# Selective-scan strand of a four-layer kernel: decay into PSUM, products on GpSimd, halved scans, new banks and orders

## The chip, the cores and the metric

One Trainium2 chip, one core. The metric is the device time of one execution in microseconds, median of the runs shown. TensorE is PE in the rows, VectorE DVE, ScalarE ACT, GpSimd POOL, and SP issues the DMAs. All arithmetic is in float32, except the rows that add a bias in a product (bfloat16 parts).

## The reference, cut to what matters

Four layers in a row over x of 32 batches x 256 steps x 256 channels. L0 and L3 are linear attention with FiLM, L1 is softmax attention with 16 heads of 16, and L2 has two selective scans, the second over reversed time:

```python
delta = softplus(einsum(dlt, Wdt) + bdt)              # batch, 256 steps, 512 channels
dA  = exp(delta[..., None] * A)                       # ... x 16 states
dBu = delta[..., None] * Bm[:, :, None, :] * u[..., None]
def step(h, xs):                                      # one step of time
    h = dA_t * h + dBu_t
    y = einsum('ben,bn->be', h, C_t)
...
out = einsum((y1 + y2) * silu(mx), Wf) + bf + skip
return x + gate * out
```

A, dBu and y are what the change touches: 2 scans x 512 channels x 16 states x 256 steps per batch, 32 batches.

## The kernel before, in words

A setup part turns the weights once (until about 150 us). Then one block runs 32 batches as four strands, each a generator per engine whose `yield` ends a step:

- **A** (L0, then L1; `pe_linear`, `pe_softmax` and their like on each engine) is one serial chain per batch. L1 makes scores of two heads at a time ("s0" to "s7", L368), VectorE takes their maxima (L425), then the scores come again transposed ("st0" to "st7", L389), ScalarE takes exponentials (L466) and TensorE multiplies with v (L398). A has PSUM banks 0 to 2 and one buffer A_x.
- **C** (first half of L2; `c_pe`, `c_dve`, `c_act`, `c_pool`): norms, projections, softplus; L559 finishes delta, L658 makes delta * u. It stores delta and delta * u in DRAM (dd) and B and C rows (bc). Banks 3 and 4.
- **S** (the scans; `s_*`). The loads of `load_slot` bring dd back, each channel on four partitions. A batch has 32 units u = (channel block c of 4, direction s of 2, q of 4); a unit is 128 partitions (32 channels x 4 states) by 4 lines of 256 steps. Per unit: ScalarE writes the decay exp(delta * A) to the buffer S_dA, 255 of 256 elements per line so that a zero stays where a line starts (four instructions, L682); VectorE writes the product B * (delta * u) to PSUM banks 6 and 7 (L702) and scans all 1024 elements in one instruction to the buffer X (L710); GpSimd multiplies X by C in place (L730), once VectorE is past the B product of the next unit; TensorE sums over states into bank 5 (L751). After 8 units VectorE gates the sum (L719). X has four places.
- **T** (end of L2, then L3; `t_*`): the product with wf, L786 and L790 on VectorE, then L3 as L0. It uses buffers of C (dd, xh, tmp) and so waits in `last_c` for C of two batches later. Banks 3 and 4, shared with C.

Each engine has one written list of letters, ORDER (L906), which is one turn: `program` (L915) takes one step of the strand that each letter names. In a turn A works on batch b + 2, C on b + 1, S on b and T on b - 1. Engines execute their lists in order, and semaphores hold them together. All DMAs are issued by SP in a list of its own.

L275 is the last write of a layer: A_x<-ps,A_ring ends L0, A_x<-ps,A_x ends L1, xs<-ps,xs ends L3.

## Time and profile before

| | |
|---|---|
| three runs | 5470.70, 5474.84, 5478.48 us (median 5474.84) |
| span of the profiled execution | 5460.8 us |
| what lies around the span, against the median | 14 us |
| busy: PE, PEld, DVE | 4205.5, 2715.4, 4723.7 us |
| busy: ACT, POOL | 3712.5, 3038.3 us |
| mean granted TensorE clock | 0.814 |

The profiled execution's own time is given as its span, from the first to the last instruction. Busy shares count instructions that run; matmuls are pipelined, so a busy PE is not PE at its peak. A float32 matmul has two records. An idle time in a row is charged to the instruction that ended the wait.

### The profile page before, as it was taken

How to read it: one execution, taken by the hardware profiler on the slowest of the kernel's cores; microseconds unless marked ns; L12 is line 12 of the kernel's file. 1: busy time of each engine (PE TensorE's matmuls, PEld its weight loads, DVE VectorE, ACT ScalarE, POOL GpSimd, SP SyncE). 2: the span in 40 equal slices, each digit the busy share in tenths (PEclk: the TensorE clock that was granted, in tenths of full speed). 3: DMA queues.
4: the chain of work that ended last, by engine and by line, in shares of the span. 5: the costliest groups of instructions: out<-in, count | busy, mean ns of one | idle time of the engine just before them, and what ended most of it. 6: DMA issues, size and time to landing. Idle time of an engine off the chain costs nothing.

```text
span 5460.8 us, 71238 instructions
## 1 busy us (share of the span) xinstructions
PE 4205.5 (77%) x25876; PEld 2715.4 (50%) x25876; DVE 4723.7 (87%) x4533; ACT 3712.5 (68%) x8614; POOL 3038.3 (56%) x1388
## 2 busy tenths in 40 slices
PE   5677787788878877888787778878877888788655
PEld 4444455555545555555455555555555555455423
DVE  4217999999999999999999999999999999999986
...
DMA packets 321199, 462.13 MB, mean 85 GB/s; under 512 B 55457, under 2 KB 148777, under 8 KB 320845
## 3 DMA queue, kind: packets, MB, share of 16 engines
...
q14 instruction: 150, 1.23, 0.1%
...
## 4 chain that ended last, share of the span: by engine, by line
PE 42%; DVE 40%; issue 6%; ACT 6%; POOL 3%; DVEq 0%; DMA 0%; SPq 0%; POOLq 0%; ACTq 0%
PE ps L164 21%; DVE S_X L710 20%; DVE ps L702 10%; PE ps L751 5%; PE ps L389 4%; PE ps L368 4%; DVE A_sm L425 3%; PE ps L524 3%; POOL S_X L730 3%; PE ps L154 2%; ACT S_dA L682 2%; DVE A_raw L129 1%; PE ps L398 1%; DVE T_raw L129 1%; ACT A_ring L147 1%
## 5 line engine op out<-in xcount | busy, mean ns | idle before, releaser
L730 POOL TENSOR_TENSOR S_X<-S_X,S_bc 128x1024 f32<-128x1024 f32 x1024 | 2442.5, 2386 | 1738.5 <-DVE ps L702 1738.3
L710 DVE TENSOR_TENSOR_SCAN S_X<-S_dA,ps 128x1024 f32<-128x1024 f32 x1024 | 2337.8, 2283 | 73.1 <-PE ps L751 1.0
L682 ACT ACTIVATE S_dA<-S_slot,acol 128x255 f32<-128x255 f32 x4096 | 1706.9, 495 | 275.8 <-DVE S_X L710 275.8
L702 DVE TENSOR_TENSOR ps<-S_slot,S_bc 128x1024 f32<-128x1024 f32 x1024 | 1337.3, 1306 | 27.6
L751 PE MATMUL ps<-S_X,sum 128*32 128x256 f32 x8192 | 732.9, 463 | 76.6 <-POOL S_X L730 73.7
L154 PE MATMUL ps<-ident,A_ring 128*128 128x128 f32 x768 | 189.7, 405 | 486.6 <-ACT A_ring L147 375.3
L751 PEld LDWEIGHTS ps<-S_X,sum 128*32 128x32 f32 x8192 | 218.2, 123 | 427.1 <-issue 253.3
L368 PE MATMUL ps<-A_kP,A_qP 32*128 32x256 f32 x2048 | 338.1, 453 | 119.1 <-DVE A_sm L425 119.1
L154 PEld LDWEIGHTS ps<-ident,A_ring 128*128 128x128 f32 x768 | 131.1, 205 | 566.0 <-ACT A_ring L147 426.5
L466 ACT ACTIVATE A_ring<-ps 128x1024 f32<-128x1024 f32 x256 | 261.5, 1021 | 188.5 <-PE ps L389 188.5
L425 DVE TENSOR_REDUCE A_sm<-ps 128x4 f32<-128x1024 f32 x256 | 311.8, 1218 | 48.6 <-PE ps L368 36.2
L389 PE MATMUL ps<-A_qP,A_kP 32*128 32x256 f32 x2048 | 335.8, 451 | 20.7 <-ACT A_ring L466 12.3
L368 PEld LDWEIGHTS ps<-A_kP,A_qP 32*128 32x128 f32 x2048 | 196.6, 207 | 251.2 <-DVE A_sm L425 192.9
L164 PE MATMUL ps<-C_xT,wcz 128*128 128x256 f32 x1024 | 296.3, 441 | 1.8 <-ACT C_dd L600 1.8
L658 POOL TENSOR_TENSOR C_dd<-C_dd 128x1024 f32<-128x1024 f32 x64 | 179.2, 2801 | 190.0 <-DVE C_dd L559 190.0
L389 PEld LDWEIGHTS ps<-A_qP,A_kP 32*128 32x128 f32 x2048 | 199.0, 209 | 144.6 <-issue 100.4
L164 PEld LDWEIGHTS ps<-C_xT,wcz 128*128 128x128 f32 x1024 | 220.6, 227 | 61.5 <-issue 12.6
L746 PE MATMUL ps<-C_xT,wD 128*128 128x256 f32 x512 | 166.1, 456 | 77.3 <-DVE S_g L719 73.2
L138 ACT ACTIVATE A_nm<-A_mv 128x2 f32<-128x2 f32 x128 | 26.0, 203 | 266.3 <-DVE A_mv L132 266.3
L164 PE MATMUL ps<-wf,S_g 128*128 128x256 f32 x512 | 198.7, 570 | 4.8 <-DVE S_X L710 2.4
L398 PE MATMUL ps<-A_ring,A_vA 128*32 128x256 f32 x2048 | 162.9, 443 | 37.8 <-ACT A_ring L466 37.8
L460 ACT ACTIVATE A_ring<-ps 16x256 f32<-16x256 f32 x32 | 11.9, 372 | 253.2 <-PE ps L375 253.2
...
## 6 DMA issues: line engine op xcount, KB each, us to landing
S_slot<-scr_dd SPq DMA_DIRECT2D x1024, 256.0 KB, 4.6
...
S_bc<-scr_bc SPq DMA_DIRECT2D x256, 256.0 KB, 5.3
...
```

The source lines that it names most:

```text
L154: ins = p.transpose(bank[:, col * 256 + r * P:col * 256 + (r + 1) * P], src[:, r, col * P:(col + 1) * P], ident[:])
L164: ins = p.matmul(out, l, r, start=n == 0, stop=n == len(terms) - 1)
L368: ins = p.matmul(bank[o][:, t * 256:(t + 1) * 256], B["qP"][r, g, t * P:(t + 1) * P], B["kP"][r, g, :], start=True, stop=True, tile_positi ...
L389: ins = p.matmul(bank[o][:, t * 256:(t + 1) * 256], B["kP"][r, g, t * P:(t + 1) * P], B["qP"][r, g, :], start=True, stop=True, tile_positi ...
L398: ins = p.matmul(bank[2][PADH * i:PADH * (i + 1), g % 2 * 256:(g % 2 + 1) * 256], B["vA"][:, t, 4 * g + i, :], B["ring"][:, 4 * (g % 2) + ...
L425: v.tensor_reduce(B["sm"][:, :, 2 * n:2 * n + 2].rearrange("p t h -> p h t"), B["pair"].rearrange("p h (t m) -> p h t m", t=TT), AX, ALU.m ...
L466: a.activation(B["ring"][:, 2 * (n % 4):2 * (n % 4) + 2, :], B["pair"], ACT.Exp).then_inc(S.act.sem, 1)
L682: ins = a.activation(B["dA"][:, s, q % 2, j, lo:lo + T - 1], B["slot"][:, s, j, 0, lo:lo + T - 1], ACT.Exp, scale=K.k["acol"][:, s, 4 * c ...
L702: v.tensor_tensor(B["in"], B["slot"][:, s, :, 1, :], rep(B["bc"][:, s, q, :], 1, 4), ALU.mult).then_inc(S.dve.sem, 1)
L710: v.tensor_tensor_scan(line(X[:, u % 4]), line(B["dA"][:, s, q % 2]), line(B["in"]), 0.0, ALU.mult, ALU.add).then_inc(S.dve.sem, 1)
L730: g.tensor_tensor(B["X"][:, u % 4], B["X"][:, u % 4], rep(B["bc"][:, s, NQ + q, :], 1, 4), ALU.mult).then_inc(S.pool.sem, 1)
L751: ins = p.matmul(B["bank"][32 * j:32 * j + 32, (c % 2) * T:(c % 2 + 1) * T], K.k["sum4"][:], B["X"][:, u % 4, j, :], start=False, stop=las ...
```

## The change

- **Scan (s_act, s_dve).** ScalarE writes the decay of half a unit (two lines of 256) straight into one of three PSUM banks (5, 6, 7), used in a ring. There is no zero column kept any more: GpSimd sets the first delta of each line to 1e30 before dd is stored (event far), and A is held at or above 3e-28, so that the exponential there is 0. VectorE scans each half by itself (512 elements).
- **Products.** GpSimd makes all 32 B products into X, now a ring of 8. In odd units (ON_POOL) VectorE scans X in place and GpSimd makes the C product over 1024 elements, queued behind the B product of two units later (POOL_LAG). In even units VectorE scans in place in the PSUM bank and makes the C product itself, 512 elements at a time, into X.
- **Banks.** A has 0 and 1, C has 2, T has 3, the state sums 4, the decay ring 5 to 7. The waits that a shared bank needs move with that. In L1 the products with v are made two groups at a time, after e3 and e7. In L0 and L3 the row sums and the reciprocal of q move ahead of y.
- **T** has buffers of its own; `last_c` is gone.
- **Orders.** The strands run on over all batches (`batches`), each engine's list is a long FIRST and then a repeated TURN. A turn has 100 steps of S on VectorE, 24 of A, 11 of T and 4 of C; on GpSimd 48, 2, 1 and 8. In VectorE's FIRST the 100th step of S, the last of batch 0, stands behind 2.83 batches of A's steps, one batch of C's and none of T's; the same distances hold at the end of each S.
- S_sp and s_sp wait for GpSimd's b instead of VectorE's, and the load of bc for the last sum instead of the last C product. The number of DMAs stays.

Core of the diff:

```diff
 UNITS, SLOTS = 32, 8
+LINES, RING, SCAN_BANKS = 4, 8, 3
+ON_POOL = frozenset(range(1, UNITS, 2))
+GATE_LAG, POOL_LAG = 2, 2
+FAR = 1e30
 ACT_SET = "natural_log_exp_and_others"
-
-AHEAD = {"A": 2, "C": 1, "S": 0, "T": -1, "a": 3, "s": 1, "t": -1}
...
-BANKS = {"L0": {"xT": 0, "q": 1, "k": 2, "v": 0, "kT": 2, "qT": 1, "att": 0, "y": 2, "hT": 1, "o": 0},
-         "L1": {"hT": 2, "o": 0},
-         "L3": {"xT": 0, "q": 1, "k": 0, "v": 1, "kT": 0, "qT": 1, "att": 0, "y": 1, "hT": 0, "o": 1}}
+BANKS = {"L0": {"xT": 0, "q": 1, "k": 0, "v": 1, "kT": 0, "qT": 1, "att": 0, "y": 1, "hT": 0, "o": 1},
+         "L1": {"hT": 0, "o": 1},
+         "L3": {n: 0 for n in ("xT", "q", "k", "v", "kT", "qT", "att", "y", "hT", "o")}}
...
     yield
+    if L == "L3":
+        p.wait_ge(S.dve.sem, S.dve.at(b, "qsub"))
     for c in range(KD):
         ins = matmuls(p, bank["k"][:, c * 256:(c + 1) * 256], [(k[L + "wk"][:, i, c * P:(c + 1) * P], B["xT"][:, i, :]) for i in range(KD)]
                       + [(k["bias"][:, K.at[L + "k"]][:, c * P:(c + 1) * P], B["om" + L][:])])
     ins.then_inc(S.pe.sem, 1)
     yield
     if L == "L3":
+        p.wait_ge(S.act.sem, S.act.at(b, "kexp1"))
+    else:
         p.wait_ge(S.dve.sem, S.dve.at(b, "qsub"))
     project(p, bank["v"], B["xT"], k[L + "wv"], bias("v"), k["ones"], S.pe)
     yield
-    p.wait_ge(S.act.sem, S.act.at(b, "kn1" if L == "L0" else "kexp1"))
+    p.wait_ge(S.act.sem, S.act.at(b, "kn1" if L == "L0" else "v1"))
     turn_tiles(p, k["ident"], B["ke"], bank["kT"], S.pe)
     yield
...
-    p.wait_ge(S.act.sem, S.act.at(b, "kT"))
+    H = P // dh
+    p.wait_ge(S.act.sem, S.act.at(b, "qT"))
+    for t in range(TT):
+        for c in range(KD):
+            at = 256 + (t * KD + c) * H
+            p.matmul(bank["att"][:, at:at + H], B["xT"][:, c, t * P:(t + 1) * P], k["same%d" % dh][:, 0:P:dh], start=True, stop=True)
     lhs, rhs = (B["v"], B["kT"]) if L == "L0" else (B["kT"], B["v"])
     for c in range(KD):
         ins = matmuls(p, bank["att"][:, c * P:(c + 1) * P], [(lhs[:, t, c * P:(c + 1) * P], rhs[:, t, c * P:(c + 1) * P]) for t in range(TT)])
     ins.then_inc(S.pe.sem, 1)
     yield
-    p.wait_ge(S.dve.sem, S.dve.at(b, "bd1"))
-    p.wait_ge(S.act.sem, S.act.at(b, "qT"))
+    p.wait_ge(S.dve.sem, S.dve.at(b, "qrec"))
     for t in range(TT):
         for c in range(KD):
             ins = p.matmul(bank["y"][:, t * D + c * P:t * D + (c + 1) * P], B["xT"][:, c, t * P:(t + 1) * P], B["bd"][:, c, :], start=True, stop=True)
-
-    H = P // dh
-    for t in range(TT):
-        for c in range(KD):
-            at = 256 + (t * KD + c) * H
-            ins = p.matmul(bank["att"][:, at:at + H], B["xT"][:, c, t * P:(t + 1) * P], k["same%d" % dh][:, 0:P:dh], start=True, stop=True)
...
+            bk = bank[1 - half]
             for c in range(2):
                 f = slice((2 * half + c) * P, (2 * half + c + 1) * P)
                 last = (k["bias"][:, K.at["L1" + m]][:, f], k["ones"][:] if m == "q" else B["omL1"][:])
                 ins = matmuls(p, bk[:, c * 256:(c + 1) * 256], [(k[L + "w" + m][:, i, f], B["xT"][:, i, :]) for i in range(KD)] + [last])
             ins.then_inc(S.pe.sem, 1)
     yield
-    p.wait_ge(S.act.sem, S.act.at(b, "q1"))
-    project(p, bank[2], B["xT"], k[L + "wv"], k["bias"][:, K.at[L + "v"]], k["ones"], S.pe)
+    p.wait_ge(S.dve.sem, S.dve.at(b, "k0"))
+    project(p, bank[1], B["xT"], k[L + "wv"], k["bias"][:, K.at[L + "v"]], k["ones"], S.pe)
 
     for n in range(PAIRS):
         yield
         p.wait_ge(S.dve.sem, S.dve.at(b, "m%d" % (n - 1) if n else "k1"))
+        if n == 0:
+            p.wait_ge(S.act.sem, S.act.at(b, "v1"))
...
-    for n in range(PAIRS + 1):
-        if n < PAIRS:
+    for n in range(PAIRS):
+        yield
+        if n == 0:
+            p.wait_ge(S.act.sem, S.act.at(b, "max"))
+            p.wait_ge(K.land["max"].sem, K.land["max"].at(b))
+        else:
+            p.wait_ge(S.act.sem, S.act.at(b, "yT0" if n == 4 else "e%d" % (n - 1)))
+        for t in range(TT):
+            for g, i, o in heads(n):
+                r = slice(PADH * i, PADH * (i + 1))
+                ins = p.matmul(bank[o][:, t * 256:(t + 1) * 256], B["kP"][r, g, t * P:(t + 1) * P], B["qP"][r, g, :],
+                               start=True, stop=True, tile_position=(PADH * i, 0))
+        ins.then_inc(S.pe.sem, 1)
+        if n % 4 == 3:
             yield
-            if n == 0:
-                p.wait_ge(S.act.sem, S.act.at(b, "max"))
-                p.wait_ge(K.land["max"].sem, K.land["max"].at(b))
...
-            for t in range(TT):
-                for i in range(4):
-                    ins = p.matmul(bank[2][PADH * i:PADH * (i + 1), g % 2 * 256:(g % 2 + 1) * 256], B["vA"][:, t, 4 * g + i, :],
-                                   B["ring"][:, 4 * (g % 2) + i, t * 256:(t + 1) * 256], start=t == 0, stop=t == TT - 1,
-                                   tile_position=(0, PADH * i), skip_group_check=True)
+            p.wait_ge(S.act.sem, S.act.at(b, "e%d" % n))
+            for g in (n // 2 - 1, n // 2):
+                for t in range(TT):
+                    for i in range(4):
+                        ins = p.matmul(bank[0][PADH * i:PADH * (i + 1), g % 2 * 256:(g % 2 + 1) * 256], B["vA"][:, t, 4 * g + i, :],
+                                       B["ring"][:, 4 * (g % 2) + i, t * 256:(t + 1) * 256], start=t == 0, stop=t == TT - 1,
+                                       tile_position=(0, PADH * i), skip_group_check=True)
             ins.then_inc(S.pe.sem, 1)
...
         g.tensor_tensor(B["dd"][:, :, 1, :], B["dd"][:, :, 1, :], B["dd"][:, :, 0, :], ALU.mult).then_inc(S.pool.sem, 1)
+        g.wait_ge(S.pool.sem, S.pool.at(b, "du%d" % s))
+        g.memset(B["dd"][:, :, 0, (T - 1) * s:(T - 1) * s + 1], FAR).then_inc(S.pool.sem, 1)
...
 def s_act(a, K, b):
     S, B = K.S["S"], K.Sb
     for u in range(UNITS):
-        yield
-        m, c, s, q = u // 4, u // 8, (u // 4) % 2, u % 4
-        lo = 1 - s
-        if q == 0:
-            a.wait_ge(K.land["slot%d" % s].sem, K.land["slot%d" % s].at(b, 4 * (c + 1)))
-        if q >= 2:
-            a.wait_ge(S.dve.sem, S.dve.at(b, "scan%d" % (u - 2)))
-        elif u >= 6:
-            a.wait_ge(S.dve.sem, S.dve.at(b, "scan%d" % (u - 6)))
-        elif b:
-            a.wait_ge(S.dve.sem, S.dve.at(b - 1, "scan%d" % (u - 6 + UNITS)))
-        for j in range(4):
-            ins = a.activation(B["dA"][:, s, q % 2, j, lo:lo + T - 1], B["slot"][:, s, j, 0, lo:lo + T - 1], ACT.Exp, scale=K.k["acol"][:, s, 4 * c + j, q:q + 1])
-        ins.then_inc(S.act.sem, 1)
+        c, s, q = u // 8, (u // 4) % 2, u % 4
+        for i in range(2):
+            yield
+            if q == 0 and i == 0:
+                a.wait_ge(K.land["slot%d" % s].sem, K.land["slot%d" % s].at(b, 4 * (c + 1)))
+            before = 2 * (UNITS * b + u) + i - SCAN_BANKS
+            if before >= 0:
+                bb, ub, ib = before // (2 * UNITS), before // 2 % UNITS, before % 2
+                a.wait_ge(S.dve.sem, S.dve.at(bb, ("scan%d_%d" if ub in ON_POOL else "c%d_%d") % (ub, ib)))
+            for n in range(2):
+                j = 2 * i + n
+                ins = a.activation(B["bank"][half_at(b, u, i)][:, n * T:(n + 1) * T], B["slot"][:, s, j, 0, :], ACT.Exp,
+                                   scale=K.k["acol"][:, s, LINES * c + j, q:q + 1])
+            ins.then_inc(S.act.sem, 1)
 
 
 def s_dve(v, K, b):
     S, B = K.S["S"], K.Sb
-    X = B["X"]
-    for w in range(UNITS + 2):
+    two = lambda ap: ap.rearrange("p (j t) -> p j t", t=T)
+    for w in range(UNITS + GATE_LAG):
         if w < UNITS:
             u, c, s, q = w, w // 8, (w // 4) % 2, w % 4
-            line = lambda ap: ap.rearrange("p j t -> p (j t)")[:, ::-1] if s else ap.rearrange("p j t -> p (j t)")
+            line = lambda ap: ap[:, ::-1] if s else ap
+            for i in range(2):
+                decay, x = B["bank"][half_at(b, u, i)], B["X"][:, u % RING, 2 * i:2 * i + 2, :]
+                out = x.rearrange("p j t -> p (j t)") if u in ON_POOL else decay
+                yield
+                if i == 0:
+                    v.wait_ge(S.pool.sem, S.pool.at(b, "b%d" % u))
+                v.wait_ge(S.act.sem, S.act.at(b, "exp%d_%d" % (u, i)))
+                v.tensor_tensor_scan(line(out), line(decay), line(x.rearrange("p j t -> p (j t)")), 0.0, ALU.mult, ALU.add).then_inc(S.dve.sem, 1)
+                if u not in ON_POOL:
+                    yield
+                    if u in (0, 4):
+                        v.wait_ge(K.land["bc%d" % s].sem, K.land["bc%d" % s].at(b))
+                    v.wait_ge(S.dve.sem, S.dve.at(b, "scan%d_%d" % (u, i)))
+                    v.tensor_tensor(x, two(decay), rep(B["bc"][:, s, NQ + q, :], 1, 2), ALU.mult).then_inc(S.dve.sem, 1)
+        if w >= GATE_LAG and (w - GATE_LAG) % 8 == 7:
             yield
...
 def s_pool(g, K, b):
     S, B = K.S["S"], K.Sb
-    for u in range(UNITS):
-        yield
-        s, q = (u // 4) % 2, u % 4
-
-        g.wait_ge(S.dve.sem, S.dve.at(b, "b%d" % (u + 1) if u + 1 < UNITS else "scan%d" % u))
-        g.tensor_tensor(B["X"][:, u % 4], B["X"][:, u % 4], rep(B["bc"][:, s, NQ + q, :], 1, 4), ALU.mult).then_inc(S.pool.sem, 1)
+    for w in range(UNITS + POOL_LAG):
+        if w < UNITS:
+            u, c, s, q = w, w // 8, (w // 4) % 2, w % 4
+            yield
+            if q == 0:
+                g.wait_ge(K.land["slot%d" % s].sem, K.land["slot%d" % s].at(b, 4 * (c + 1)))
+            if u in (0, 4):
+                g.wait_ge(K.land["bc%d" % s].sem, K.land["bc%d" % s].at(b))
+            if u >= RING:
+                g.wait_ge(S.pe.sem, S.pe.at(b, "sum%d" % (u - RING)))
+            elif b:
+                g.wait_ge(S.pe.sem, S.pe.at(b - 1, "sum%d" % (u - RING + UNITS)))
+            g.tensor_tensor(B["X"][:, u % RING], B["slot"][:, s, :, 1, :], rep(B["bc"][:, s, q, :], 1, LINES), ALU.mult).then_inc(S.pool.sem, 1)
+        u = w - POOL_LAG
+        if u in ON_POOL:
+            s, q = (u // 4) % 2, u % 4
+            yield
+            g.wait_ge(S.dve.sem, S.dve.at(b, "scan%d_1" % u))
+            g.tensor_tensor(B["X"][:, u % RING], B["X"][:, u % RING], rep(B["bc"][:, s, NQ + q, :], 1, LINES), ALU.mult).then_inc(S.pool.sem, 1)
...
-        p.wait_ge(S.pool.sem, S.pool.at(b, "c%d" % u))
+        if u in ON_POOL:
+            p.wait_ge(S.pool.sem, S.pool.at(b, "c%d" % u))
+        else:
+            p.wait_ge(S.dve.sem, S.dve.at(b, "c%d_1" % u))
...
-def last_c(e, K, b):
-
-    S, c = K.S["C"], min(b + 2, NB - 1)
-    e.wait_ge(S.pool.sem, S.pool.at(c, "gate"))
-    e.wait_ge(K.land["dd_out1"].sem, K.land["dd_out1"].at(c))
-
-
```

BANKS of L0, `dve_softmax` and `act_softmax` follow the banks above. C waits for the copy out of its one bank ahead of each product; the first product of T waits for the end of the T before. The strings of FIRST and TURN are left out.

## Rows read from the trace of the kernel before

**Rows 1.** The page, busy time, share of the span and instructions of each engine.

```profile
PE 4205.5 (77%) x25876; PEld 2715.4 (50%) x25876; DVE 4723.7 (87%) x4533; ACT 3712.5 (68%) x8614; POOL 3038.3 (56%) x1388
```

**Rows 2.** Busy us (instructions) of PE, PEld, DVE, ACT, POOL by stretch; clock, DMA, GB/s.

```profile
620.00:2190.00 1570.00, 1261.31 (x7940) 816.15 (x7940) 1444.83 (x1351) 1156.73 (x2691) 949.34 (x431) 0.84 0.38 89
2190.00:3760.00 1570.00, 1259.21 (x7941) 816.09 (x7941) 1445.76 (x1351) 1157.13 (x2690) 949.71 (x431) 0.84 0.38 89
```

**Rows 3.** Line L275 between 2300 and 2800 us: ns min/median/max, first and last start.

```profile
L275 DVE TENSOR_TENSOR A_x<-ps,A_x x4: 691/692/692, 2309.3 to 2780.3; 128x512 f32<-128x512 f32 x4
```

**Rows 4.** Line L275 over the whole span.

```profile
L275 DVE TENSOR_TENSOR A_x<-ps,A_x x32: 690/692/693, 300.3 to 5135.5; 128x512 f32<-128x512 f32 x32
L275 DVE TENSOR_TENSOR xs<-ps,xs x32: 691/691/693, 736.5 to 5457.6; 128x512 f32<-128x512 f32 x32
```

**Rows 5.** Timeline of VectorE (start us, us, engine, line): three single writes.

```profile
434.72 0.69 DVE L275 TENSOR_TENSOR A_x<-ps,A_x 128x512 f32<-128x512 f32 x1 [12.08 <-PE ps L164]
...
5282.21 0.69 DVE L275 TENSOR_TENSOR xs<-ps,xs 128x512 f32<-128x512 f32 x1 [0.17 <-PE ps L164]
...
5411.49 0.69 DVE L275 TENSOR_TENSOR xs<-ps,xs 128x512 f32<-128x512 f32 x1 [0.59 <-PE ps L164]
```

**Rows 6.** The page, chain of work that ended last, by engine and by line.

```profile
PE 42%; DVE 40%; issue 6%; ACT 6%; POOL 3%; DVEq 0%; DMA 0%; SPq 0%; POOLq 0%; ACTq 0%
PE ps L164 21%; DVE S_X L710 20%; DVE ps L702 10%; PE ps L751 5%; PE ps L389 4%; PE ps L368 4%; DVE A_sm L425 3%; PE ps L524 3%; POOL S_X L730 3%; PE ps L154 2%; ACT S_dA L682 2%; DVE A_raw L129 1%; PE ps L398 1%; DVE T_raw L129 1%; ACT A_r
```

**Rows 7.** The page, costliest groups: count, busy us, mean ns, idle before and releaser.

```profile
L730 POOL TENSOR_TENSOR S_X<-S_X,S_bc 128x1024 f32<-128x1024 f32 x1024 | 2442.5, 2386 | 1738.5 <-DVE ps L702 1738.3
L710 DVE TENSOR_TENSOR_SCAN S_X<-S_dA,ps 128x1024 f32<-128x1024 f32 x1024 | 2337.8, 2283 | 73.1 <-PE ps L751 1.0
L702 DVE TENSOR_TENSOR ps<-S_slot,S_bc 128x1024 f32<-128x1024 f32 x1024 | 1337.3, 1306 | 27.6
L466 ACT ACTIVATE A_ring<-ps 128x1024 f32<-128x1024 f32 x256 | 261.5, 1021 | 188.5 <-PE ps L389 188.5
```

**Rows 8.** Who waited for whom, VectorE: us in total, times, longest.

```profile
DVE A_x L275 <- PE ps L164: 158.2, 64, 12.1
DVE C_xh L786 <- PE ps L164: 93.0, 31, 8.1
```

**Rows 9.** Single lines of VectorE over the span: ns min/median/max.

```profile
L702 DVE TENSOR_TENSOR ps<-S_slot,S_bc x1024: 1204/1232/3183, 435.3 to 5406.2; 128x1024 f32<-128x1024 f32 x171
...
L710 DVE TENSOR_TENSOR_SCAN S_X<-S_dA,ps x1024: 2266/2286/2290, 437.3 to 5408.6; 128x1024 f32<-128x1024 f32 x171
...
L790 DVE TENSOR_TENSOR xs<-xs,C_xh x32: 691/692/693, 682.5 to 5423.4; 128x512 f32<-128x512 f32 x32
```

**Rows 10.** Single lines of GpSimd, and its groups by form.

```profile
L730 POOL TENSOR_TENSOR S_X<-S_X,S_bc x1024: 2336/2357/3352, 441.0 to 5411.0; 128x1024 f32<-128x1024 f32 x171
...
L658 POOL TENSOR_TENSOR C_dd<-C_dd x64: 2343/2368/3281, 346.3 to 5215.5; 128x1024 f32<-128x1024 f32 x64
...
L1469 POOL MEMSET const-float32-1.0<- 128x1 f32 x1 | 0.1, 99 | 0.0
```

**Rows 11.** Timeline: four exponentials of ScalarE.

```profile
2509.71 1.70 ACT L682 ACTIVATE S_dA<-S_slot,acol 128x255 f32<-128x255 f32 x4 [0.45 <-DVE S_X L710]
```

**Rows 12.** Strand A undisturbed: stretches of L1 and L0, and its timeline.

```profile
207.00:300.00 93.00, 58.54 (x270) 34.66 (x270) 14.45 (x21) 19.62 (x35) 1.26 (x1) 0.59 0.01 3
300.00:336.00 36.00, 24.95 (x105) 18.83 (x104) 8.13 (x25) 19.56 (x53) 6.82 (x6) 0.74 0.05 16
...
224.27 0.84 ACT L456 ACTIVATE A_vA<-ps,A_pc 128x256 f32<-128x256 f32 x2 [5.25 <-PE ps L164]
260.19 2.07 PE L389 MATMUL ps<-A_qP,A_kP 32*128 32x256 f32 x8 [1.12 <-ACT A_ring L466]
262.19 1.93 PE L398 MATMUL ps<-A_ring,A_vA 128*32 128x256 f32 x16
264.06 2.08 PE L389 MATMUL ps<-A_qP,A_kP 32*128 32x256 f32 x8
```

More of the change, by code:

```diff
@@ L1 @@
 from contextlib import ExitStack
+from itertools import chain, cycle
 import concourse.bass as bass
@@ L347, in pe_softmax @@
     turn_tiles(p, k["ident"], B["xh"], bank[0], S.pe)
-    for m, bb in (("q", (1, 2)), ("k", (0, 1))):
+    for m in "qk":
         for half in range(2):
             yield
-            p.wait_ge(S.act.sem, S.act.at(b, "q0" if m == "k" and half else "xT"))
-            bk = bank[bb[half]]
+            p.wait_ge(S.act.sem, S.act.at(b, "q%d" % half if m == "k" else "xT"))
+            bk = bank[1 - half]
             for c in range(2):
@@ L417, in dve_softmax @@
     norm_stats(v, lambda t: x[:, t, :], B["st"], S.dve, b, [("", 0), ("", 1)])
-    for half, bk in ((0, bank[0]), (1, bank[1])):
+    for half, bk in ((0, bank[1]), (1, bank[0])):
         yield
@@ L932, in products_of_setup, with batches @@
+def batches(e, K, make):
+    for b in range(NB):
+        yield from make(e, K, b)
+def program(e, K, engine):
+    work = {letter: batches(e, K, make) for letter, make in WORK[engine].items()}
+    for strand in work.values():
+        next(strand)
+    running, order = set(work), chain(FIRST[engine], cycle(TURN[engine]))
+    while running:
+        letter = next(order)
+        if letter in running and next(work[letter], "over") == "over":
+            running.remove(letter)
 def products_of_setup():
@@ L1393, in buffers @@
     A["omL0"], A["omL1"] = sb("omL0", [P, T], BF16), sb("omL1", [P, T], BF16)
[L1394 removed]
+    A["bank"] = [ps[:, b, :] for b in (0, 1)]
     A["pair"] = ps[:, 0:2, :]
@@ L1432, in _ @@
             def _(v):
-                for q in range(2):
-                    v.memset(K.Sb["dA"][:, 0, q, :, 0:1], 0.0).then_inc(K.ready, 1)
-                    v.memset(K.Sb["dA"][:, 1, q, :, T - 1:T], 0.0).then_inc(K.ready, 1)
                 v.memset(K.A["vA"][:], 0.0).then_inc(K.ready, 1)
```

413 lines of the change are left out of this document (294 added, 119 removed).

## The prediction

> **What bounds the kernel now.** I read five views, in this order. First the busy shares [rows 1]: VectorE 87%, TensorE 77%, ScalarE 68%, GpSimd 56%. Then the busy time by stretch [rows 2]: from 620 us on, two stretches of ten turns have the same VectorE time to a microsecond, 1444.8 and 1445.8 of 1570, so a turn (one batch in each of the four strands) has one fixed length, with VectorE busy 144.5 us of it. Its length stands in the writes of x [rows 3]: four from 2309.3 to 2780.3 us, 157.0 apart. The first final output is at 736.5, the last at 5457.6 [rows 4, 5]; between them lie 28 turns of 157 (4396), then 149, 129 and 46 us, where strands have run out.
>
> The chain of waits [rows 6] says what makes a turn 157 long: 42% TensorE and 40% VectorE, of that 20% the scan L710 and 10% the product L702. This is strand A (L0 and L1 of one batch, a serial chain), standing behind scans. Last the costs by line [rows 7]: a turn has 32 scans of 2.283 and 32 B products of 1.306, 73.1 + 41.8 = 114.9 us; VectorE's other work is 144.5 - 114.9 = 29.7. The short idle times ahead of L710 and L702 are (73.1 + 27.6)/32 = 3.1. So 157 = 144.5 + 3.1 + 9.4; the 9.4 is mostly VectorE standing in its fixed order before a product of TensorE that has not come: two of its lines, L275 and L786, waited 158.2 + 93.0 us in the span for TensorE, 8 per turn [rows 8].
>
> **The change, part by part.**
>
> *VectorE.* It loses the 32 B products. It makes 64 half scans and 32 half C products (16 even units). No row has a scan of 512. A product takes 1.232 for 1024 elements and 0.692 for 512 [rows 4, 9], so 0.15 fixed and 1.05 ns per element; the same fixed part on a scan gives (2.283 + 0.15)/2 = 1.217. Ends: 1.142 (nothing fixed) and 1.30 (twice as much fixed), which is -5 and +5 us per turn. I take 1.217, since every VectorE group of two sizes has that fixed part. Sum: 64 x 1.217 + 32 x 0.692 + 29.7 = 77.9 + 22.1 + 29.7 = 129.7, where 144.5 was. Hand-overs: 96 operations instead of 64, of which 32 wait for the scan just before them; at 71 ns for one ahead of a dependent L710 that is 3.1 to 7, and I take 4.
>
> Operands in PSUM: the scan's decay now comes from PSUM and its other input from SBUF, before the other way round. A product with one input in PSUM (L275) and one with both in SBUF (L790) both take 0.692 [rows 4, 9], so I put nothing on it. The Trainium skill, "VectorE: DVE Perf Modes", section on the TRN2 errata, gives 58 cycles of fixed cost to an SBUF source and 120 to a PSUM source. By that rule the 32 C products, which read PSUM where the B products did not, would cost 65 ns more each (an estimate from the page, 2.1 us per turn, some 60 us in all); the two rows disagree with it.
>
> *VectorE against GpSimd.* B product L702 has median 1.232, mean 1.306 and a worst case of 3.183 [rows 7, 9]; L658 on GpSimd goes from 2.343 to 3.281 [rows 10]. L710, with one SBUF input, has 2.266 to 2.290 throughout [rows 9], and the C products of GpSimd that start beside one have a median of 2.357. So a VectorE instruction with two SBUF inputs and a GpSimd instruction hold each other up, one with a single SBUF input does not. The change takes the 32 two-input products away, and halves and C products have one SBUF input each. What stays is three per turn (L559 twice, L790), and GpSimd will almost always be busy then: up to one GpSimd operation (2.36) each, 0 to 7 us per turn, half of it 3.5. The Trainium skill, "SBUF — State Buffer", section "Who interferes with whom", has the same rule, as an exclusive lock on the shared port pair for the whole instruction; by it alone the price would be that of the whole lock, up to 7.
>
> *GpSimd.* 32 B products and 16 C products of 2.357 (median of L730 [rows 10]) are 113.1. Its other work is 95.0 - 32 x 2.386 = 18.6 now [rows 2, 7], where 95.0 is 949.7/10, less 1 that L658 gets back with the collisions, 17.6. The two new memsets are 0.1 each, by a small memset row [rows 10]; the other end is half a product, 1.2. Together 130.9, where 95 was. It becomes as full as VectorE.
>
> *ScalarE.* 128 exponentials of 256 instead of 255 elements; four take 1.70 now, 0.425 each [rows 11], and 1024 elements out of PSUM take 1.02 [rows 7], so between 0.26 and 0.43 at the new place. I keep 0.425 and 115.7 per turn [rows 2]; less would change nothing, since ScalarE has 30 us to spare. New is the cover: dA gave ScalarE two units or more, over 7 us; the ring of three halves lets it be at most two halves ahead, 2.4 to 3.8 us. L466 stood 188.5/32 = 5.9 us per turn behind TensorE [rows 7]; an exponential queued behind it now can be late. Bounds 0 to 5.9; I take it inside the remainder below.
>
> *TensorE and banks.* Same products, 126 us of records per turn [rows 2]. Strand A goes from three banks to two. In the undisturbed L1 of batch 0 (93 us, granted clock 0.59) [rows 12]: s0 now also waits for the v copy, +1.0. A step of st and e takes 2.08 + 1.02 + 0.1 = 3.2; with a group of y between (260.19 to 264.06) it takes 3.87, so a group cost 0.67 three times and its whole 1.93 at the end, 3.9. Now two groups come together after e3 and again after e7, 3.8 each, and yT0 (half of 1024 elements, 0.6) stands before st4: 8.2 - 3.9 = +4.3. A is 5 us longer. In L0 q's reciprocal and the row sums move ahead of y, out of the way (1 us less), and v and att wait longer for their bank (about as much): nothing. C on one bank adds eight alternations of about 1 us, T (L3) about 6 us. The last T, alone, takes 46 us [rows 4, 5], and C of batch 0 fits between 300 and 435 us beside an A; both have a whole turn, so nothing. T no longer shares C's buffers and no longer waits for C of two batches later; that can give back some of L786's 93/32 = 2.9 us per turn (0 to 2.9, I take 0). *SP queue:* same DMAs. The slot loads now wait for GpSimd's b instead of VectorE's and are wanted about four units (16 us) later. Nothing.
>
> *The sum for a turn:* VectorE 129.7 + hand-overs 4 + collisions 3.5 = 137.2, plus the remainder of 9.4 as it is = 146.6, less 0.6 for scans half as long in front of A: **146 us**. Start: A of batches 0 and 1 ends at 434.7 [rows 5], plus 10 for two longer As. The new VectorE list puts 83% of A's third batch ahead of the end of the first S, as the old one put all of it: 0.83 turn. Then one turn to the first output, 28 more, and the last three. S of batch 30 without A is bound by GpSimd (131 less A's two products) at 130, S of batch 31 (113 and T's product) at 118; the last T is 47. For turn length t: 434.7 + 10 + 29.83 t + 130 + 118 + 47 + 3 (output) + 14 = 757 + 29.83 t. The 14 is what lies around the span: 5474.8 is the median, the profiled span 5460.8. With t = 157 and no other gain this gives 5440 for 5475, because the last three stretches are shorter. With t = 146: **5112 us**, 6.6% less.
>
> **The rivals.**
> (a) *Well packed.* The remainder vanishes since scans are half as long and T is free of C: t = 138, 4874 us. For it: strand A alone takes 93 + 36 = 129 [rows 12] at a low clock, less at 0.84. Against it: VectorE 137, GpSimd 131 and A 134 would all have to fit in 138.
> (b) *Strand A is the bound.* A needs 129 + 5 by itself and waited 28 in a turn; with GpSimd's queue full and ScalarE's cover thin, only 10 of the 28 go: t = 152, 5291 us. For it: 42% of the chain on TensorE, which the change does not touch.
> (c) *GpSimd and VectorE in lockstep: slower.* GpSimd's C product waits for a scan and stands in its queue ahead of the next B, which VectorE needs; the lag is two units, 7 us. If none of GpSimd's other work (17.6) is hidden by that lag, all of it becomes idle VectorE: t = 146 + 17.6 = 163.6, 5637 us. It turns slower than now from 12.5 of the 17.6 on (t = 158.5). For it: GpSimd is at 131 of 146 and can't catch up. Against: A's reductions slow VectorE, not GpSimd, and the new lists interleave C singly.
> (d) *It brings nothing:* ring or slots starve the scan so that t stays at 157 to 158. By the shorter end alone that is 5440 to 5470 us, 0.6% faster to the same.
>
> **How the numbers follow.** Forecast 0.58 (own range t = 142 to 150: 4993 to 5232), (a) 0.15, (b) 0.18, (c) 0.06, (d) 0.03. The ends of the unknown costs (half scan -5 to +5, hand-overs -1 to +3, collisions -3.5 to +3.5, cover 0 to +5.9, T -2.9) make 138.5 to 153 if not all fall on one side: 4885 to 5325. Runs spread by 0.14%, so 0.2% is what can be told from no change. Faster 0.92 (all but (c) and a part of (d)), same 0.02, slower 0.06.
>
> **What would show it.** Half scans of 1.22 and half C products of 0.69, both steady beside GpSimd; 2.36 for B; writes of x 146 apart; VectorE at 89 to 91% and GpSimd at 88 to 90% of a turn. (a) would show as x 138 apart; (b) as VectorE idle before A's steps behind TensorE and ScalarE; (c) as VectorE idle before scans with GpSimd as the releaser; (d) with ScalarE. I would be wrong by the largest amount if GpSimd's idle time before C products and VectorE's before scans both pass 10 us per turn, or if the half scan costs over 1.3.

## The result, and the profile after

Median 5265.3 us (5261.9 to 5271.6) against 5472.8 (5463.1 to 5478.5): a ratio of 0.962, 95% interval 0.961 to 0.964. The change brings 207 us where 363 were forecast; the time lies in the stated range (4885 to 5325), outside the forecast's own range (4993 to 5232), and near rival (b)'s 5291. Below, a "turn" is the mean distance of the writes of x by strand A, from the 6th to the 32nd, in the profiled execution. Times are medians of four runs, and a_alone has a single one. One run of pe_off_chain, 9632 us at a granted clock of 0.634 where the other three have 0.815 to 0.819, is left out.

The page of the kernel after answers [rows 1, 6 and 7]: busy time by engine, the chain that ended last, and the costly groups. L711 is the scan (once for even, once for odd units), L717 VectorE's C product, L744 B and L750 C on GpSimd, L692 the exponentials, L774 the sums.

```profile
PE 4086.9 (78%) x25876; PEld 2626.4 (50%) x25876; DVE 4162.8 (79%) x5553; ACT 3681.6 (70%) x8614; POOL 4130.8 (79%) x1964
...
PE 46%; ACT 21%; DVE 13%; POOL 7%; issue 7%; DMA 2%; SPq 1%; DVEq 0%; POOLq 0%; ACTq 0%
```

```profile
L744 POOL TENSOR_TENSOR S_X<-S_slot,S_bc 128x1024 f32<-128x1024 f32 x1024 | 2396.2, 2361 | 70.7 <-DMA S_bc<-scr_bc 27.6 <-DMA S_slot<-scr_dd 25.1 <-issue 17.6
L692 ACT ACTIVATE ps<-S_slot,acol 128x256 f32<-128x256 f32 x4096 | 1731.5, 466 | 223.6 <-DVE S_X L717 183.0 <-DVE S_X L711 27.4 <-DMA S_slot<-scr_dd 9.2
L711 DVE TENSOR_TENSOR_SCAN ps<-ps,S_X 128x512 f32<-128x512 f32 x1024 | 1249.4, 1220 | 170.2 <-ACT ps L692 121.9 <-POOL S_X L744 47.6
L750 POOL TENSOR_TENSOR S_X<-S_X,S_bc 128x1024 f32<-128x1024 f32 x512 | 1218.4, 2380 | 370.3 <-DVE S_X L711 308.9 <-DMA S_bc<-scr_bc 60.2
L711 DVE TENSOR_TENSOR_SCAN S_X<-ps,S_X 128x512 f32<-128x512 f32 x1024 | 1206.6, 1206 | 53.0 <-ACT ps L692 49.4 <-POOL S_X L744 2.3 <-POOL S_X L750 0.4
L717 DVE TENSOR_TENSOR S_X<-ps,S_bc 128x512 f32<-128x512 f32 x1024 | 703.1, 687 | 34.3 <-issue 0.2
```

The busy time of two stretches of some ten turns each (as [rows 2]), and the writes of x (as [rows 4]):

```profile
1062.00:2586.00 1524.00, 1229.89 (x7948) 790.01 (x7946) 1272.75 (x1670) 1146.17 (x2688) 1289.99 (x611) 0.85 0.40 92
2586.00:4087.00 1501.00, 1215.31 (x7952) 778.87 (x7952) 1272.67 (x1674) 1147.10 (x2697) 1293.22 (x612) 0.86 0.40 93
```
```profile
L282 DVE TENSOR_TENSOR A_x<-ps,A_x x32: 666/691/693, 318.9 to 4983.9; 128x512 f32<-128x512 f32 x32
```

The two stretches are 1524 and 1501 us long: the turn now varies (146 to 161), where it was 157.0 each time [rows 3]; its mean is 150.8. That makes 20.06 turns of the 3025 us, each with VectorE busy 126.9 us, GpSimd 128.8, TensorE 121.9 and ScalarE 114.3. VectorE works 17.6 us less per turn than before and the turn is only 6.2 shorter: its idle time grew from 12.5 to 23.9. The chain has only 13% of VectorE (40% before [rows 6]), 7% of GpSimd, and 46% of TensorE.

Where VectorE's new idle time stands (waited for, us in total between 1062 and 4984 us, which is 26 turns, times, longest):

```profile
DVE S_g L726 <- PE ps L774: 140.5, 40, 8.3
DVE ps L711 <- ACT ps L692: 108.4, 84, 3.6
DVE A_sm L432 <- PE ps L377: 87.4, 113, 3.3
DVE S_X L711 <- ACT ps L692: 35.0, 36, 4.3
```

Of some 23.6 us per turn, 13.1 lie ahead of strand S's own steps (3.1 before): 5.5 are scans that wait for exponentials and 5.4 the gate L726 that waits for TensorE's sums. 8.3 lie ahead of A's steps (4.2 before).

The written orders differ too. The kernel before repeats one list each turn. The kernel after runs all 32 batches on TensorE and VectorE out of FIRST, and cut after each last step of S there, no two neighbouring turns are alike. The change thus also put irregular orders in place of a regular one; new_order below bears on that.

### The profile page after: what moved, and what is told of

The parts are those of the page before. It is cut to its first block, busy times and chain, and to the rows that moved or that the text cites. A ratio compares the mean times of both kernels' runs of the same rounds, so it can differ in the third digit from the quotient of the medians.

```text
span 5260.2 us, 72771 instructions
## 1 busy us (share of the span) xinstructions
PE 4086.9 (78%) x25876; PEld 2626.4 (50%) x25876; DVE 4162.8 (79%) x5553; ACT 3681.6 (70%) x8614; POOL 4130.8 (79%) x1964
## 4 chain that ended last, share of the span: by engine, by line
PE 46%; ACT 21%; DVE 13%; POOL 7%; issue 7%; DMA 2%; SPq 1%; DVEq 0%; POOLq 0%; ACTq 0%
PE ps L170 23%; ACT ps L692 6%; PE ps L774 5%; PE ps L396 5%; PE ps L377 4%; DVE ps L711 4%; POOL S_X L744 3%; DVE S_X L711 3%; POOL S_X L750 3%; ACT A_ring L471 2%; PE ps L405 2%; PE ps L529 2%; ACT A_ring L153 2%; PE ps L766 1%; DVE S_X L717 1%
## 5 line engine op out<-in xcount | busy, mean ns | idle before, releaser
L744 POOL TENSOR_TENSOR S_X<-S_slot,S_bc 128x1024 f32<-128x1024 f32 x1024 | 2396.2, 2361 | 70.7 <-DMA S_bc<-scr_bc 27.6
L692 ACT ACTIVATE ps<-S_slot,acol 128x256 f32<-128x256 f32 x4096 | 1731.5, 466 | 223.6 <-DVE S_X L717 183.0
L750 POOL TENSOR_TENSOR S_X<-S_X,S_bc 128x1024 f32<-128x1024 f32 x512 | 1218.4, 2380 | 370.3 <-DVE S_X L711 308.9
L711 DVE TENSOR_TENSOR_SCAN ps<-ps,S_X 128x512 f32<-128x512 f32 x1024 | 1249.4, 1220 | 170.2 <-ACT ps L692 121.9
L711 DVE TENSOR_TENSOR_SCAN S_X<-ps,S_X 128x512 f32<-128x512 f32 x1024 | 1206.6, 1206 | 53.0 <-ACT ps L692 49.4
L774 PE MATMUL ps<-S_X,sum 128*32 128x256 f32 x8192 | 704.6, 453 | 125.3 <-POOL S_X L750 118.2
L717 DVE TENSOR_TENSOR S_X<-ps,S_bc 128x512 f32<-128x512 f32 x1024 | 703.1, 687 | 34.3 <-issue 0.2
L396 PE MATMUL ps<-A_qP,A_kP 32*128 32x256 f32 x2048 | 391.4, 513 | 197.7 <-ACT A_ring L471 97.8
L774 PEld LDWEIGHTS ps<-S_X,sum 128*32 128x32 f32 x8192 | 218.2, 121 | 464.9 <-issue 215.3
L396 PEld LDWEIGHTS ps<-A_qP,A_kP 32*128 32x128 f32 x2048 | 231.2, 241 | 365.1 <-ACT A_ring L471 170.0
L160 PE MATMUL ps<-ident,A_ring 128*128 128x128 f32 x768 | 141.2, 319 | 326.1 <-ACT A_ring L153 320.0
L377 PE MATMUL ps<-A_kP,A_qP 32*128 32x256 f32 x2048 | 302.7, 414 | 55.7 <-DVE A_sm L432 50.3
L662 POOL TENSOR_TENSOR C_dd<-C_dd 128x1024 f32<-128x1024 f32 x64 | 150.8, 2357 | 191.3 <-DVE C_dd L563 191.3
L377 PEld LDWEIGHTS ps<-A_kP,A_qP 32*128 32x128 f32 x2048 | 182.2, 191 | 161.4 <-DVE A_sm L432 84.7
L726 DVE SCALAR_TENSOR_TENSOR S_g<-ps,bD,wa 128x256 f32<-128x256 f32 x128 | 60.1, 469 | 174.5 <-PE ps L774 174.3
L170 PE MATMUL ps<-A_ring,L1wq 128*128 128x256 f32 x512 | 180.9, 493 | 13.5 <-ACT A_ring L455 13.2
## 6 DMA issues: line engine op xcount, KB each, us to landing
T_gate<-scr_mod SPq DMA_DIRECT2D x32, 128.0 KB
```

The costliest lines, as they stand in the source:

```text
L160: ins = p.transpose(bank[:, col * 256 + r * P:col * 256 + (r + 1) * P], src[:, r, col * P:(col + 1) * P], ident[:])
L170: ins = p.matmul(out, l, r, start=n == 0, stop=n == len(terms) - 1)
L377: ins = p.matmul(bank[o][:, t * 256:(t + 1) * 256], B["qP"][r, g, t * P:(t + 1) * P], B["kP"][r, g, :], start=True, stop=True, tile_positi ...
L396: ins = p.matmul(bank[o][:, t * 256:(t + 1) * 256], B["kP"][r, g, t * P:(t + 1) * P], B["qP"][r, g, :], start=True, stop=True, tile_positi ...
L692: ins = a.activation(B["bank"][half_at(b, u, i)][:, n * T:(n + 1) * T], B["slot"][:, s, j, 0, :], ACT.Exp, scale=K.k["acol"][:, s, LINES * ...
L711: v.tensor_tensor_scan(line(out), line(decay), line(x.rearrange("p j t -> p (j t)")), 0.0, ALU.mult, ALU.add).then_inc(S.dve.sem, 1)
```

## Where a turn goes, counted along strand A

For this one view I took all records of TensorE, ScalarE, VectorE and GpSimd that touch A's tiles and laid them end to end: the time in which some engine works on A, and between two such times the gap ahead of A's next instruction. In a gap its engine is either busy for another strand (A stands behind it) or idle. Over some 24 to 26 turns of each trace, per turn:

```
                     before   after   new_order (below)
turn                  157.0   151.1   146.8
A worked on           106.9   111.6   114.1
A behind TensorE       24.2    21.0    18.4
A behind VectorE       12.2     4.7     5.7
A behind ScalarE        4.8     6.8     3.4
A behind GpSimd         1.5     0.5     0.2
gaps, engine idle       7.4     6.6     5.0
```

In both kernels A is always at work or next in a queue whose engine is busy, but for 7 us. By itself this does not show that A is the bound, since the parts add up to the turn for any strand. The same count along strand S, from the same records of the kernel after, gives 141.1 worked on, 8.3 behind others and 1.5 idle. What the count gives is prices, which the experiments can test. The change took 7.5 us of standing behind VectorE's scans and B products, 3.2 behind TensorE and 1.0 behind GpSimd, put 2.0 on behind ScalarE, and A's own work grew by 4.7; idle gaps lost 0.8. That is -5.8, the whole of the gain. Of the 4.7, 1.7 is TensorE's own time on A (57.5 to 59.2) and 3.0 is overlap between engines that is gone. One place from TensorE's and ScalarE's timelines of the kernel after (start, length):

```profile
3012.88 1.60 PE L396 MATMUL ps<-A_qP,A_kP 32*128 32x256 f32 x8
3014.41 3.72 PE L170 MATMUL ps<-wf,S_g 128*128 128x256 f32 x16
3017.97 1.03 PE L766 MATMUL ps<-C_xT,wD 128*128 128x256 f32 x4
3018.93 1.93 PE L405 MATMUL ps<-A_ring,A_vA 128*32 128x256 f32 x32
```
```profile
3014.53 1.03 ACT L471 ACTIVATE A_ring<-ps 128x1024 f32<-128x1024 f32 x1 [2.46 <-PE ps L396]
```

A's exponentials are ready at 3015.56; the product y (L405) starts at 3018.93, since strand T's first product and strand S's L766 stand ahead of it. No "wait" shows this: TensorE is busy all the time.

## The experiments

Theories: (1) A's chain with its queueing sets the turn; (2) GpSimd and VectorE in lockstep; (3) TensorE's total work; (4) the ring of three halves. All kernels start from the kernel after. The first five leave work out, in turn on A, on VectorE, on GpSimd, on ScalarE, and on the last three together. Turns come from one profiled execution, times from the median, and the two can differ: over 29.83 turns, 1 us per turn is 30 us.

**a_half.** `B["pair"]...[:, :, :, 0:128]` in the maxima, `ring[..., 0:256] <- pair[..., 0:256]` in the exponentials, and both halves of y read `ring[..., 0:256]`.

> The kernel after, with strand A's eight maxima (L1) over 512 instead of 1024 elements and its eight exponentials over 512 instead of 1024, so half of the keys are left out; TensorE's products, all orders and all other strands are as they are. This takes 8 x 0.61 + 8 x 0.45 = 8.5 us per turn out of A's serial chain, 4.9 of it from VectorE's work and 3.6 from ScalarE's. Theory 1 (A's chain sets the turn): the turn falls from 150.8 by 6 to 9 us, time 4997 to 5086 us. Theory 2 (GpSimd and VectorE in lockstep through scans and B products): GpSimd's 130 us are not touched, VectorE's only by 4.9, so 0 to 4.9 us per turn, 5119 to 5265 us. Theory 3 (TensorE's own work and queue): 0, 5250 to 5270 us.

Measured 5176.9 us (0.947 of before, 0.945 to 0.949), turn 148.3: 2.5 of the 8.5 us come off. Theory 3 falls (the turn moves with TensorE's work unchanged). The size misses theory 1 and lies in theory 2's range, so this run alone does not decide between them; the next two do. That A gives less than its own saving is seen along A: standing behind TensorE rose from 21.0 to 25.3.

**dve_light and pool_light.**

```
-  v.tensor_tensor_scan(line(out), line(decay), line(x), 0.0, ...)
+  v.tensor_tensor_scan(line(out[:, 0:T]), line(decay[:, 0:T]), line(x[:, 0:T]), 0.0, ...)
```
```
-  g.tensor_tensor(X[:, u % RING], X[:, u % RING], rep(bc, 1, LINES), ALU.mult)
+  g.tensor_tensor(X[:, u % RING, 0:2], X[:, u % RING, 0:2], rep(bc, 1, 2), ALU.mult)
```

> The kernel after, with each half scan over one of its two lines (256 elements instead of 512), the other line left unscanned; nothing else is changed. VectorE's work falls by 64 x 0.54 = 34 us per turn, from 127 to 93; A's chain has no scan in it, only stands behind some. Theory 1 (A's chain): the turn falls only by what A's VectorE steps waited for the scan ahead of them, 0 to 5 us, 5116 to 5265 us. Theory 2 (lockstep): GpSimd's C products wait 309 us in the span for scans, 10 per turn, and the turn can come down to GpSimd's 131 plus a few: 134 to 142 us, 4760 to 5000 us. Theory 3 (TensorE): 5200 to 5265.

> The kernel after, with the C products of GpSimd over two of their four lines (512 elements instead of 1024), the other two left out. GpSimd's work falls by 16 x 1.1 = 18 us per turn, from 130 to 112. Theory 1 (A's chain): 0 to 3 us per turn, 5175 to 5265 us. Theory 2 (lockstep): most of GpSimd's 18 us come off the turn, 10 to 18, 4730 to 4970 us. Theory 3 (TensorE): 5200 to 5265.

Measured 5200.1 us, turn 149.4: VectorE's busy time fell by 32 us per turn, worth 1.4 (2.2 by the medians); and 5234.3 us, turn 149.8: GpSimd's fell by 17, worth 1.0. Nearly half of the scans' work gone and 99% of the turn left: neither engine alone is the bound. Both times also lie in theory 3's range, so they say nothing against TensorE.

**act_light.** One exponential for both lines: `a.activation(bank as (2, 256), slot[:, s, j:j + 2, 0, :], Exp, scale=acol of line j)`.

> The kernel after, with one exponential of 512 elements for each half (the second line takes the first one's factor) instead of two of 256: ScalarE's 64 x 2 x 0.466 become 64 x about 0.72, 13 us per turn less of 115, and each half is ready 0.2 us sooner. Theory 1 (A's chain, with ScalarE's A steps standing behind exponentials): 1 to 4 us per turn, 5146 to 5235 us. Theory 4 (the ring of three halves: scans that wait for exponentials, 171 us in the span, set the turn): 4 to 6 us per turn, 5086 to 5146 us. Theories 2 and 3: 5235 to 5265.

Measured 5187.3 us, turn 148.5: 2.3 us per turn, theory 1's range; theory 4 asked for 4 to 6. Along A, standing behind ScalarE fell from 6.8 to 4.4, which is all of it. ScalarE's busy time fell by 11 us. This is the thin cover that the prediction put at nothing.

**three_light.** The three together.

> The kernel after, with dve_light, pool_light and act_light together: VectorE 93, GpSimd 112, ScalarE 102 us per turn, TensorE and strand A as they are. Theory 1 (A's chain with TensorE's queue): three engines freed by 13 to 34 us each give no more than what A stood behind them; alone two of them gave 2.2 and 1.0 us per turn, together 4 to 9: 4997 to 5146 us. Theory 2 (lockstep of any two or three of VectorE, GpSimd and ScalarE, which no single one of them frees): 15 us per turn or more, under 4820 us.

Measured 5066.0 us, turn 146.2: 4.6 us per turn, the sum of the three alone (1.4 + 1.0 + 2.3 = 4.7). The profiled execution is the slowest of the four here (5086); by the medians it is 6.7, against 5.8 for the sum. Either way no pair of them holds the turn jointly: 62 us of the three engines' busy time are gone, and the 15 us or more that theory 2 asked for do not come. Theory 2 falls.

**pe_on_chain, pe_off_chain.** Less TensorE work, once inside A (one of two terms in A's `project` and q, k products, `for t in range(1)` in y), once outside (`if j % 2: continue` in the sums, one of two terms in wcz and wx).

> The kernel after, with less TensorE work on strand A's chain: its projections q, k, v and o (L0 and L1) over one of two halves of the contraction, the products y of L1 over one of two halves of the keys. By the groups of the profile after this takes 466/32 = 14.6 us per turn of TensorE out, all of it in A. Theory 1 (A's chain): the turn falls by a third of that or more, as when A's maxima and exponentials were halved (8.5 us out of A gave 3.0 per turn), 5 to 12 us: 4907 to 5116 us. Theory 2 (VectorE and GpSimd in lockstep): 0 to 1, 5235 to 5265. Theory 3 (TensorE's work in all, wherever it is): as much as pe_off_chain by the microsecond.

> The kernel after, with less TensorE work outside strand A: two of the four sums of each unit left out (strand S), the products with wcz and wx over one of two halves of the contraction (strand C). By the groups of the profile after this takes 552/32 = 17.3 us per turn of TensorE out, none of it in A. Theory 1 (A's chain): only what A's products stood behind others in TensorE's order, 0 to 4 us per turn, 5146 to 5265 us. Theory 3 (TensorE's work in all): 17.3/14.6 of what pe_on_chain gains. Theory 2 (lockstep): 0 to 1, 5235 to 5265.

Measured 5144.2 us, turn 147.5 (3.3 for 14.6 us) and 5192.2 us, turn 148.3 (2.5 for 17.3 us). By the work left out, a microsecond is worth 0.23 on the chain and 0.14 off it (0.28 and 0.14 by the medians). The first is outside theory 1's range; part of the reason is that the granted clock fell with the work, from 0.835 to 0.802 over the span (0.818 in pe_off_chain). TensorE's busy time on the two pages is 3866.2 and 3969.7 us for 4086.9: only 221 of 466 us and 117 of 552 really went. By that measure a microsecond of TensorE is worth no more on the chain (0.48) than off it (0.68), and in both places more than one of any other engine. Theory 3 as it stands is out by a_half, but that TensorE's queue as a whole, and not A's part of it, weighs most is not excluded.

**a_light.** a_half and pe_on_chain together.

> The kernel after, with a_half and pe_on_chain together: 8.5 + 14.6 = 23.1 us per turn out of strand A's chain (half of the elements of its maxima and exponentials, half of the contraction of its projections and y products); the other strands as they are. Theory 1 (A's chain sets the turn, other engines only where A stands behind them): the two gains add, 3.0 + 4.1 = 7.1 us per turn or more: 4980 to 5080 us. Rival (below about 146 the turn is held by VectorE with GpSimd, as the forecast had it): the second gain is mostly lost, 3.5 to 5 us in all, 5115 to 5160 us.

Measured 5047.2 us, turn 144.6: 6.2 us per turn, where the two alone gave 2.5 + 3.3. They add up, and by the medians too (7.3 against 3.0 + 4.1); 23 us taken out of A move the turn more than 62 us taken out of the three others, 218 us of time against 199. But they are 23 us by count: the time in which A is worked on fell by 17.4, to 94.1, and its standing behind other strands rose by 11. The rival (VectorE with GpSimd holds at 146) falls.

**a_alone.** Only strand A in the table of strands, x written out from A.

> Strand A alone (L0 and L1 of all 32 batches, written out as they are): strands C, S and T are left out, so nothing stands in any queue ahead of A. It shows how long one A takes when undisturbed. Setup ends near 170 us. Theory 1 (A is the bound): 125 to 140 us per batch, so 32 of them take 4180 to 4660 us in all; the 151 of the kernel after would hold only 11 to 26 us of waiting for other strands. Theory 2 (lockstep of the others) or 3 (TensorE's total): A alone takes under 115 us, under 3850 us in all, and has over 35 us of slack in a turn. The granted clock can be lower than beside the other strands; what this costs is to be read from TensorE's rows.

Measured 4553.8 us. Line L282 and a stretch of it (busy by engine, granted clock):

```profile
L282 DVE TENSOR_TENSOR A_x<-ps,A_x x32: 690/692/692, 310.3 to 4548.8; 128x512 f32<-128x512 f32 x32
```
```profile
1000.00:4000.00 3000.00, 1759.52 (x7693) 1116.56 (x7692) 464.25 (x831) 697.57 (x1445) 55.49 (x44) 0.60 0.02 4
```

(4548.8 - 310.3)/31 = 136.7 us for one A at a granted clock of 0.60; the prediction had 129 + 5, at 0.59 in L1 and 0.74 in L0. TensorE's part of it is 79.5 us here and 59.2 beside the other strands at 0.86, so an undisturbed A at that clock would take about 116 (an estimate from the two traces). A waits some 35 us per turn, not 17. The time is in theory 1's range, but read at that clock the run does not decide: 116 and 35 of slack are about what theories 2 and 3 asked for.

**pool_lag3.** `GATE_LAG, POOL_LAG = 2, 3`.

> The kernel after, whole computation, with GpSimd's C product of a unit put three units behind its B product instead of two, in the same places of the order. Theory 2 (lockstep: GpSimd stands 309 us in the span before C products for scans): this wait goes, 2 to 8 us per turn, 5030 to 5205 us. Theory 1 (A's chain): the wait moves elsewhere on GpSimd or becomes idle time, and sums on TensorE come 3.6 us later: 5235 to 5300 us.

Measured 5426.9 us (0.993 of before), turn 156.6: 5.7 us longer, almost the whole gain lost, and more than any theory gave. Who waits for GpSimd's C product, in the kernel after and here (us, times, longest):

```profile
PE ps L774 <- POOL S_X L750: 118.2, 57, 8.1
```
```profile
PE ps L774 <- POOL S_X L750: 319.1, 136, 9.6
```

The 200 us more are 6.3 per turn of TensorE standing at a sum, in order. Along A, idle gaps grew by 2.6 per turn, nearly all of them on TensorE, standing behind TensorE by 1.7 and A's own work by 1.5. GpSimd's own wait for scans did go, as theory 2 said (309 to 128 us), and it was worth nothing.

**a_split.** Whole computation; each step of A's L1 becomes two of one bank, so that TensorE writes bank 1 while VectorE or ScalarE reads bank 0.

```
-  for t in range(TT):
-      for g, i, o in heads(n): matmul(bank[o][...t...])
-  ins.then_inc(S.pe.sem, 1)
+  for g, i, o in heads(n):
+      wait m(n - 1, o)
+      for t in range(TT): matmul(bank[o][...t...])
+      ins.then_inc(S.pe.sem, 1)
```

> The kernel after, whole computation, with each step of A's L1 (scores of two heads in two banks, one maximum or exponential over both) made as two steps of one bank each, in the same place of every order: TensorE fills bank 1 while VectorE or ScalarE reads bank 0. VectorE's work grows by 8 x 0.15 = 1.2 us per turn, ScalarE's by 8 x 0.2 = 1.6, TensorE's is the same or a little more. Theory 1 (A's chain): a step alone falls from about 3.2 us to 2.3 or so, 16 steps; with other strands' instructions queued between, a part of these 14 us: 4 to 11 us per turn, 4937 to 5146 us. Theory 2 (lockstep of GpSimd and VectorE): VectorE is 1.2 us fuller, 5265 to 5300. Theory 3 (TensorE's work): 5265 to 5290.

Measured 5252.9 us (0.960, 0.959 to 0.962), turn 151.1: 12 us faster in all, none of it in the turn, and in no theory's range. The scores of A's L1 in the kernel after and here:

```profile
L396 PE MATMUL ps<-A_qP,A_kP 32*128 32x256 f32 x2048 | 391.4, 513 | 197.7 <-ACT A_ring L471 97.8 <-DMA A_qP<-A_ring 79.0 <-ACT A_kP L476 18.8
```
```profile
L396 PE MATMUL ps<-A_qP,A_kP 32*128 32x256 f32 x2048 | 440.7, 510 | 144.8 <-DMA A_qP<-A_ring 78.0 <-ACT A_ring L473 47.8 <-ACT A_kP L478 17.3
```

One record takes as long as before and the group takes 49 us more (L377 29 more): two heads' products that alternated between banks ran partly at once, and in this order they do so less. Along A, the overlap between engines grew by some 3 us per turn and the engines' work on A by as much (2.3 of it TensorE's), so that its length stayed (111.5 and 111.9).

**new_order.** Whole computation, no instruction changed; only the written orders.

```
-  FIRST = {"PE": "...ASATCATSCSSSASCCASCASASAASAASCASTCACSACS...", ...}
+  FIRST = {"PE": "...AACSACATCSSTACSCACSSTSASAAAAACSACSACSSACS...", ...}
```

> The kernel after, whole computation, not an instruction changed, added or removed: only the five written orders in which the strands' steps are issued are new. They are made by giving each engine, whenever it is free, the step that could start first by the durations of the profile after, with 0.26 us of preference for strand A on VectorE, 0.46 on ScalarE and 1.4 on GpSimd, and 0.2 against strand T on VectorE. Theory 1 (a turn is A's own 111.6 us and what A stands behind other strands' steps, 39.6 in the kernel after, which is a matter of the orders): the standing falls by 8 to 16 us per turn, until GpSimd's 130 and VectorE's 127 busy us leave little room: turn 135 to 143, time 4790 to 5030 us. Rival (the busy engines' shared load makes A stand behind others however it is ordered): the turn stays at 148 to 154, 5180 to 5360 us. If orders made from mean durations do not survive the spread of the real ones, it is slower than the kernel after.

Measured 5139.3 us (0.940, 0.938 to 0.942): 2.4% faster than the kernel after, the fastest here. Its chain and a stretch of ten turns:

```profile
PE 29%; POOL 22%; DVE 16%; ACT 14%; issue 8%; DMA 6%; SPq 2%; POOLq 0%; ACTq 0%; DVEq 0%
```
```profile
1041.00:2509.00 1468.00, 1269.89 (x7942) 799.85 (x7941) 1276.75 (x1672) 1151.76 (x2691) 1299.22 (x611) 0.84 0.41 95
```

All turns are within 0.5 us of 146.8, and standing and idle gaps along A fell from 39.6 to 32.6, so how long A stands depends on the orders. Time and turn lie between the ranges of theory 1 (135 to 143) and the rival (148 to 154), and neither is borne out: the standing fell by 7, where 8 to 16 were expected. These orders repeat one turn, where those of the kernel after differ from turn to turn; whether the repetition or the new places gave the 2.4% was not separated. TensorE's busy time rose from 121.9 to 127.0 per turn at a clock of 0.84, and what else keeps the turn at 146.8 was not separated either.

## Why the prediction was right, and where it was short

The time lies in the stated range, and largely by luck. The range reached 5325 because unit costs might all come out high. None of VectorE's and GpSimd's did. What came was more idle time on VectorE, which the sum held constant.

- *VectorE 129.7 + 3.5 for collisions:* 126.9 measured. The half scan took 1.22 and 1.21 (1.217 forecast), the half C product 0.687 (0.692). *Hand-overs 4:* the idle time ahead of scans and C products that no other engine ended is 1.1 per turn. With it VectorE comes to 128.0, where the sum had 137.2.
- *Operands in PSUM, nothing:* right for the forecast's purpose. The 65 ns that follow for a PSUM source from the Trainium skill, "VectorE: DVE Perf Modes", TRN2 errata (an estimate from its cycles), do not show in full: the C product, with one, has a median of 0.691, and L806, with both inputs in SBUF, 0.664, which is 27 ns less.
- *Collisions 3.5 us:* too much, some 0.2. The place was right: on VectorE only the instructions with two SBUF inputs stretch (L563 to a maximum of 2.873, L806 to 2.448, against 1.232 at most for the scan), but L563's mean is 1.251 for a median of 1.215 (two per turn), L806's 0.771 for 0.664 (one). So the rule of "SBUF — State Buffer", "Who interferes with whom", in the Trainium skill fits this trace, and its price here is next to nothing.
- *GpSimd 130.9:* 128.8; *ScalarE 115.7:* 114.3. Both right.
- *A is 5 us longer:* 4.7 along A. The size is right; 1.7 of it is TensorE's own time on A, which the forecast did not have.
- *The formula 757 + 29.83 t:* with t = 150.8 it gives 5255 for 5265, but by errors that cancel. The first output came at 677.3 us, 43 earlier than it says; the 28 turns of outputs behind it were 152.2 long, 40 us more; and the last three outputs took 317 us, not 295.
- *The step that failed: "plus the remainder of 9.4 as it is".* It took VectorE as the bound and its idle time as a constant. Measured, the remainder is 150.8 - 128.0 = 22.8, 13.4 more; that VectorE's own terms were forecast 9.2 too high hid the larger part of it. dve_light shows that VectorE's work does not set the turn of the kernel after. Along A, standing behind VectorE gave 7.5, the rest gave 5.0, own work took 4.7 and ScalarE 2.0; VectorE's idle time grew by what is left of the 17.6, most of it ahead of strand S's steps. The "cover" of ScalarE, costed at nothing inside the remainder, is those 2.0. That A and not VectorE bound the kernel before as well is read from the count; no run tests it.
- *Rival (b)* had the mechanism and nearly the number (152 for 150.8): "only 10 of the 28 go". Along A 50.1 us of gaps became 39.6, 10.5 less. It was given 0.18 for want of a count along A, with the chain's 42% of TensorE in its favour. Its base was off: it put A alone at 134 at the low clock and the wait at 28. Of its sign, VectorE idle before A's steps, 8.3 of the 23.6 us are there.
- *Rival (c)*, the lockstep, is refuted by pool_light, dve_light and three_light, and pool_lag3, which takes most of its wait away, is slower.
- *What stays open:* A's chain as the bound is the account that fits most runs. But 8.5 us out of A gave 2.5 to 3.0, the rest turned into standing behind others, and the orders, TensorE's queue as a whole and A's own length were not separated from each other.
